# A graph network on one core: when the node table's SBUF copy and the last pass's first adjacency blocks are loaded

## What is computed

```python
# edges: src, dst, sorted by dst
x = x + L0(relu(layernorm(x)), ...)                        # filtered messages
x = x + L1(relu(layernorm(x)), src, dst, W, a_src, a_dst)  # attention
h = relu(layernorm(x))
# L2: graph convolution by degrees
h2  = h * rsqrt(deg_out)[:, None]
agg = segment_sum(h2[src], dst) * rsqrt(deg_in)[:, None]
x   = x + relu(agg @ W + b)
# L3: two convolutions in a row, then a weighted mean of equal copies
z = relu(layernorm(x))
for W_, b_ in ((W0, b0), (W1, b1)):
    hz = z @ W_
    z  = prelu(segment_sum(hz[src] * norm[:, None], dst) + b_, slope)
x = x + z * sum(softmax(mixing))
```

## Time and profile before

| what | value |
|---|---|
| median of 3 runs | 5152.11 us (5148.06 to 5152.26) |
| the profiled execution | 5143.11 us, span 5141.0 us, mean granted clock 0.848 |
| busy share of the span: PE, DVE, ACT, POOL | 77%, 59%, 32%, 71% |
| pass 2, first gather to first gather of pass 3 | 2951.58 to 3632.69 us |
| pass 3, likewise | 3632.69 to 4450.27 us |
| pass 4, first gather to the end | 4450.27 to 5141.0 us |

### The profile page before, as it was taken

One profiled execution on the slowest core, in us unless ns is written; L12 is line 12 of the kernel. 1 busy time (PEld: TensorE's weight loads), 2 busy tenths in 40 slices (PEclk: granted clock), 3 DMA queues, 4 the chain that ended last, 5 costly groups with the idle time before them and its releaser, 6 DMA issues.

```text
span 5141.0 us, 88720 instructions
## 1 busy us (share of the span) xinstructions
PE 3958.1 (77%) x26176; PEld 3536.6 (69%) x26176; DVE 3037.7 (59%) x11144; ACT 1656.6 (32%) x3637; POOL 3665.2 (71%) x3340
## 2 busy tenths in 40 slices
PE   2767677676766538888888788887888998698897
PEld 2656566565555537777777687777777887588886
DVE  3655555555554267777777766666555555355554
ACT  3444444444443234444444433332211111011110
POOL 0788888888888147777777467777577777577776
PEclk9877777777777868888888799999899999799998
DMA  6666666666665522222222222222444444444443
GB/s 215 136 113 117 114 117 120 111 120 114 116 112 71 113 60 56 60 60 57 57 57 57 50 69 60 59 59 59 143 138 134 134 136 151 145 153 154 156 160 104
DMA packets 412954, 541.52 MB, mean 105 GB/s; under 512 B 139471, under 2 KB 324408, under 8 KB 405944
## 3 DMA queue, kind: packets, MB, share of 16 engines
q0 software_dynamic: 199680, 221.72, 23.7%
q1 hardware_dynamic: 178524, 289.13, 17.8%
q10 hardware_dynamic: 34396, 26.36, 1.7%
HBM read 383.80 MB, written 153.13 MB: 104 GB/s over the span
## 4 chain that ended last, share of the span: by engine, by line
PE 47%; DMA 17%; issue 16%; POOL 10%; DVE 6%; ACT 2%; DVEq 1%; SPq 1%; POOLq 0%; ACTq 0%
DMA sums<-G,idx 15%; POOL sums L870 10%; PE psC L1410 9%; PE psF L1410 9%; PE psA L1331 5%; PE psD L1392 4%; PE psE L1392 4%; PE psA L1378 4%; PE psB L1378 4%; PE psC L1341 4%; DVE mc_mx L1821 1%; ACT arena L1081 1%; PE psE L1353 1%; PE psD L1346 1%; DMA stage<-table 1%
## 5 line engine op out<-in xcount | busy, mean ns | idle before, releaser
L846 POOL DMA_INDIRECT G<-table,idx x1664 | 1592.7, 957 | 626.4 <-issue 585.3
L870 POOL DMA_INDIRECT sums<-G,idx x832 | 1283.7, 1543 | 327.1 <-issue 203.2
L827 POOL DMA_INDIRECT G<-table,idx x832 | 785.7, 944 | 291.5 <-issue 269.7
L1113 ACT COPY arena<-psA 128x600 f32<-128x600 f32 x312 | 205.9, 660 | 1136.4 <-PE psA L1378 1127.0
L2229 DVE TENSOR_SCALAR S<-iota,dloc,ew 128x128 f32<-128x128 f32 x1144 | 318.0, 363 | 406.1 <-PE psE L1392 222.4
L1281 PE MATMUL psE<-arena,stage 128*128 128x128 f32 x832 | 210.8, 433 | 435.3 <-ACT G L1030 435.1
L1281 PEld LDWEIGHTS psE<-arena,stage 128*128 128x128 f32 x832 | 180.6, 320 | 519.9 <-ACT G L1030 519.9
L1410 PEld LDWEIGHTS psC<-arena,stage 128*128 128x128 f32 x3822 | 483.9, 193 | 45.0 <-issue 29.4
L1410 PE MATMUL psC<-arena,stage 128*128 128x144 f32 (+1 forms) x3822 | 493.1, 284 | 26.5 <-DMA arena<-adjacency 15.2
L1738 DVE TENSOR_TENSOR arena<-psB,G 128x1024 f32<-128x1024 f32 x104 | 127.4, 1225 | 641.8 <-PE psB L1262 641.8
L1410 PEld LDWEIGHTS psF<-arena,stage 128*128 128x128 f32 x3822 | 478.1, 191 | 15.0 <-issue 0.2
(11 more groups left out here) (293 smaller groups left out, 8105.9 us busy)
## 6 DMA issues: line engine op xcount, KB each, us to landing
adjacency<-arena SPq DMA_DIRECT2D x26, 2400.0 KB
arena<-adjacency SPq DMA_DIRECT2D x26, 2400.0 KB
acc<-in_src_row SPq DMA_DIRECT2D x104, 512.0 KB
arena<-in_dst_row SPq DMA_DIRECT2D x104, 512.0 KB
G<-table,idx POOLq DMA_INDIRECT x2496
sums<-G,idx POOLq DMA_INDIRECT x832
sums<-arena ACTq DMA_DIRECT2D x4, 3300.0 KB, 36.2
table<-cut ACTq DMA_DIRECT2D x147, 64.0 KB
```

Of the source, the lines that this page charges most:

```text
L827: pool.indirect_dma_start(G[st.r][:, t * width:(t + 1) * width], None, tables[n], bass.IndirectOffsetOnAxis(ap=idx[st.r][:, t:t + 1], axis ...
L846: pool.indirect_dma_start(G[at.r][:, t * D:(t + 1) * D], None, tables[n], bass.IndirectOffsetOnAxis(ap=idx[at.r][:, t:t + 1], axis=0)).the ...
L870: pool.indirect_dma_start(sums_dram[t % SUMS], bass.IndirectOffsetOnAxis(ap=idx[st.r][:, t:t + 1], axis=0), G[st.r][:, t * TW:(t + 1) * TW ...
L1113: A.copy(dense_at(at.g, m.loaded + j, at.place), counts_in((c * m.built + j) % 2)).then_inc(mixed["kept"], 1)
```

## The change

`stage` is loaded in four DMAs in place of one, of 12, 12, 12 and 13 row blocks, the parts that `dense_sums` reads in slots 4 to 7. Each waits only for its own rows, has a semaphore of its own, and PE waits for each part ahead of its first use. Three of them are issued ahead of the index loads of chunks 0 to 3, and the fourth where the whole load stood. In pass 4 the loads of adjacency groups 0 and 1 are issued ahead of all of these, and that of group 0 waits for one group of dense sums less (the last group reads the other buffer).

```diff
-        stage_in = Counter(h_in[0], 16 * (CHUNKS // ROWS))
+        stage_in = [Counter(h_in[q], 16 * (CHUNKS // ROWS)) for q in range(GROUP)]
...
+        def part_of(part):
+
+            return part * BLOCKS // GROUP, (part + 1) * BLOCKS // GROUP
...
                 if group < 2:
-                    sp.wait_ge(mixed["applied"], m.applied0)
+                    sp.wait_ge(mixed["applied"], m.applied0 - 1 + group)
                     sp.wait_ge(adj_moved[group], 16 * (GROUPS // 2))
...
-            def load_stage(n):
-
-                for q in range(TABLE_TILES):
-                    sp.wait_ge(table_row[q], table_rows_out(n - 1, max(range(q, BLOCKS, TABLE_TILES))))
+            def load_stage(n, parts):
+
                 if n == 2:
                     reached(sp, ns["degs"], 2)
                 else:
                     sp.wait_ge(mixed["applied"], mixes[n].applied0)
-                sp.dma_start(tiles(stage[:, 0:BLOCKS * D], BLOCKS),
-                             tables[n].rearrange("(b p) f -> p b f", p=P)).then_inc(stage_in.sem, 16)
+                for q in parts:
+                    from_, to = part_of(q)
+                    for b in range(max(to - TABLE_TILES, 0), to):
+                        sp.wait_ge(table_row[b % TABLE_TILES], table_rows_out(n - 1, b))
+                    sp.dma_start(tiles(stage[:, from_ * D:to * D], to - from_),
+                                 tables[n][from_ * P:to * P, :].rearrange("(b p) f -> p b f", p=P)).then_inc(stage_in[q].sem, 16)
 
             def near_pass(n):
                 m = mixes[n]
+                if m.loaded:
+                    load_adjacency(m, 0)
+                    load_adjacency(m, 1)
+                load_stage(n, range(GROUP - 1))
                 for c in range(CHUNKS):
...
                     if c == ROWS - 1:
-                        load_stage(n)
+                        load_stage(n, range(GROUP - 1, GROUP))
...
-                    if m.loaded and c == ROWS - 1:
-                        load_adjacency(m, 0)
-                        load_adjacency(m, 1)
-                    elif m.loaded and at.place == 0 and 0 < at.group < GROUPS - 1:
+                    if m.loaded and at.place == 0 and 0 < at.group < GROUPS - 1:
                         load_adjacency(m, at.group + 1)
...
-                        if group == 0:
-                            reached(pe, stage_in, 16 * (m.index + 1))
                         if group >= 2:
                             pe.wait_ge(mixed["spread"], m.spread((group - 1) * GROUP))
+                    if group == 0 and half_ == 0:
+                        reached(pe, stage_in[part], 16 * (m.index + 1))
```

## The result

The changed kernel takes 5122.18 us in the median of six runs (5113.98 to 5135.12), the kernel before 5152.88 in six (5148.06 to 5158.71). The ratio is 0.9944, with a 95% interval from 0.9927 to 0.9961. The forecast was 5124.7, faster.

The account below looks back on a forecast made before the run. POOL's row of gathers was taken to bound passes 2 to 4, so time cut from its standstills stays cut. Terms 4.8 + 5.0 + 17.6 = 27.4 us took the median 5152.1 to 5124.7, range 5116 to 5137.

Parts of the forecast that it names:

- What bounds: Passes 2 to 4: POOL's gathers run without a break except between passes and in one standstill per pass, together 43.2 us.
- that rival: Passes 2 to 4: something other than the standstill sets the pace, gains are given back, time 5152; chance 0.08.
- Start 3: Start of pass 3: PE's idle 3.33 us for `stage` goes, plus 1.7 us from quicker steps; 5.0 us gained.
- Start 4: Start of pass 4: PE's 15.24 us adjacency wait goes, plus 2.4 us from the clock; 17.6 us gained.
- the slower rival: Before pass 4: the load burst holds the first chunks' index loads; 5164 if the queue needs until 4490; chance 0.03.
- Start 2: Start of pass 2: PE's idle 7.97 us goes, but indices wait behind three parts; 4.8 us gained, between 3.0 and 6.7.
- indices that don't wait: Start of pass 2: index loads not held behind the parts gain 8.0 us, 3.2 us more; time 5121.5.
- The rule from the Trainium skill: Start of pass 2: fixed times of three parts in a row make indices 4 us later, gain 0.8, time 5128.7.

Follow-up runs that it names:

- the sums come first: On top of the four parts issued late, PE does a slot's gathered sums ahead of its counts and dense sums; ratio 0.9938 to the kernel before.

## Why the prediction was right

**What bounds.** The reading was that POOL's gathers run without a break but for a standstill in each pass, and that a microsecond taken from it stays taken. The standstills fell by 12.7, 5.4 and 17.4, together 35.5. Against it stands the later first gather, 6.3. That leaves 29.2, and the stretch to the end fell by 28.7. In the other kernels too the last column follows the standstills and the first gather, within 4.2 us, except where the sums come first. Nothing later gave the gain back, so that rival is out.

In one reading the forecast was short: it counted 24 waits for PE. There are 23 more, on psE, and 11 for indices, but each is a gap of 0.3 us, so that nothing changes.

**Start 3.** Forecast 5.0, measured 5.4 (10.8 to 5.4). The 3.33 us and the quicker first part are both seen.

**Start 4.** Forecast 17.6, measured 17.4 (19.7 to 2.4). The 15.24 us went, and the first part took 3.10 us. POOL's idle time ahead of pass 4 is 15.07 us where it was 15.76, and from pass 3's first gather to that of pass 4 it is 5.2 us less than before, nearly the whole 5.4 of the standstill. So the burst of 7.3 MB cost the last gathers next to nothing, and the slower rival is out with it.

**Start 2.** Forecast 4.8, measured 6.4 (21st gather 43.5 to 37.2). This is the least exact term. The forecast named the indices in line behind three parts as what POOL waits for, put the first gather 13.7 us after the degree step (12.1 measured; the value before is 5.8 and not 6.0, as the forecast had it in its last paragraph) and had no standstill left. All of that is so. What it had too small is the other delay: the table's last rows are written 3.9 us later beside the parts, where the forecast had 1.0, and only at its upper bound. In the changed kernel this is hidden, since the indices come later still. So the term came out within 1.6 us although one of its two delays was wrong, which is partly luck.

Two side remarks of the forecast were off for the same start. It said that indices that don't wait would gain 8.0. With the indices early it was 8.5 (43.5 to 35.0), near it, but not by that mechanism: POOL had no standstill there, and the late rows alone set the time. And it said that PE gains no more than its idle 7.97 us, because its clock is at the low level either way. The granted clock was 0.50 in both kernels up to PE's first dense sums, but the first 12 matmuls took 2.62 us and not 3.22, and PE reached the gathered sums of chunk 0 9.2 us earlier (32.2 us after the degree step, and 41.4 in the kernel before). POOL, which decides there, hid this too.

**The parts and the sum.** The rule from the Trainium skill (DMA: Bandwidth & Descriptors, Anatomy of one DMA and Measured), about 2 us for each DMA and 1 MiB or more, would have given 5128.7 by the estimate in the forecast. The runs don't show such a cost for loads that follow each other on SP's queue: the fourth part cost 3.05 us for 0.85 MB, 279 GB/s, near the 291 of the earlier trace rows. The sum was 27.4 forecast and 28.7 measured in the stretch. By the medians the gain is 30.7 (5152.88 to 5122.18), and the time forecast was 5124.7.

What the prediction didn't see is that half of the change to `stage` isn't needed. It took the early issue as the cause of the gain and the cuts as the means. Separate waits with a late issue, or an early issue with one wait, each do it. For the early adjacency loads no substitute was tried that does as well.

## What to carry to other kernels

Where a long load is read piece by piece, cut it and let the reader wait for each piece; then look whether issuing it earlier still brings anything, since early transfers can slow down the writes that run beside them and hold up the small loads that stand behind them. Look for the standstill of the engine that otherwise never pauses, and count what stands ahead of its release; once it is gone, the next microsecond has to come from the engine's own steps. And when two executions of one program differ by 30 us ahead of the change, compare the stretch behind a common instruction.

## What the runs showed of the hardware

- A 64 KB write on ACT's queue took 1.55 us with no load of SP beside it and about 5.5 us, from its issue to SP's next step, beside 2.4 MB of loads on SP's queue.
- Small loads on SP's queue didn't overtake large ones: 0.85 MB more ahead of a small index load delayed what waits for it by 3.05 us. Behind two adjacency loads the issuing instructions last long themselves: 17.45 us for three, where the same three took 4.13 us at start 2.
- The cut loads went in packets of about 0.5 KB, the whole load in packets of 2 KB, without a loss of rate that could be seen: 317 GB/s from 2960 to 2966 us in the changed kernel, 309 GB/s from 2953 to 2957 in the kernel before (all queues together; ACT's table rows run beside the first, four gathers beside the second). The first fence is the changed kernel, the second the kernel before:

```profile
DMA packets 3806, 1.90 MB, mean 317 GB/s; under 512 B 96, under 2 KB 3806, under 8 KB 3806
```

```profile
DMA packets 599, 1.24 MB, mean 309 GB/s; under 512 B 0, under 2 KB 0, under 8 KB 599
```

- The time up to the end of pass 1 differs between executions of the same program, 2945.8 and 2976.2 us in two profiles. The cause stays open.
